# Adaptive-norm attention and expert layer: block 0 projected first, products of zeros ahead of it, output scaled by halves of the dimensions, last expert by single tiles

## What is computed

```python
mod = (silu(c) @ wmod).reshape(4, 6, 1, 128)
sa, ca, ga, sb, cb, gb = (mod[:, i] for i in range(6))
ga = (2 * (ga >= 0) - 1) * maximum(abs(ga), 0.25)     # gb likewise
h = layernorm(x) * (1 + ca) + sa
x = x + ga * attention(h)      # 16 heads of 64, 4 k/v heads, softcap 30, window of 128 tokens
h = layernorm(x) * (1 + cb) + sb
x = x + gb * experts(h)        # 8 experts, top 1, at most 512 tokens each, 128 -> 512 -> relu -> 128, biases b1, b2
```

## Time and profile before

| | |
|---|---|
| median of 3 runs | 460.33 us (460.16 to 461.42) |
| time of the profiled execution | 464.12 us |
| its span, first to last instruction | 462.3 us |
| TensorE busy | 413.0 us, 89% of the span |
| ScalarE, GpSimd, VectorE busy | 299.7, 309.5 and 285.5 us |
| mean granted TensorE clock | 0.964 |
| granted clock, 362 to 382 and 382 to 390 us | 0.73 and 0.50 |

### The profile page before, as it was taken

How to read it: one execution, slowest core, us unless ns; L and a number is a source line. 1 busy time by engine, 2 the same in 40 slices (tenths; PEclk the granted TensorE clock), 3 DMA queues, 4 the chain that set the end, 5 groups by cost and what they waited for, 6 DMA issues and landing times. The chain is left out here.

```text
span 462.3 us, 14917 instructions
## 1 busy us (share of the span) xinstructions
PE 413.0 (89%) x5608; PEld 291.8 (63%) x5608; DVE 285.5 (62%) x846; ACT 299.7 (65%) x537; POOL 309.5 (67%) x495
## 2 busy tenths in 40 slices
PE   2889999999999999999999999999989722899980
PEld 1756666665767676676766666767656512799970
DVE  4547566766776868486776756775767651246531
ACT  3788677768786868777777868776746430564520
POOL 4444757778787878687878757786869771065573
PEclk9999999999999999999999999999999955999996
DMA  8166602000110111020202101221210046971110
GB/s 240 69 214 239 198 12 81 26 31 28 45 48 26 57 51 31 37 60 36 67 29 83 47 30 32 65 64 32 83 43 24 30 127 207 353 227 36 38 47 21
DMA packets 32494, 37.14 MB, mean 80 GB/s; under 512 B 3634, under 2 KB 28727, under 8 KB 32424
## 3 DMA queue, kind: packets, MB, share of 16 engines
q1 hardware_dynamic: 28920, 27.43, 19.4%
q0 software_dynamic: 3072, 8.37, 5.0%
q10 hardware_dynamic: 432, 0.40, 0.4%
HBM read 15.69 MB, written 16.91 MB: 71 GB/s over the span
## 5 line engine op out<-in xcount | busy, mean ns | idle before, releaser
L899 DVE COPY_PREDICATED own<-before,turns 128x1024 f32<-128x1024 uint32 x56 | 68.8, 1229 | 47.5 <-PE turns L447 47.4
L1226 POOL TENSOR_TENSOR OL<-O,OH 128x512 fp32r<-128x512 f32 x64 | 81.7, 1284 | 17.9 <-ACT OH L730 17.9
L1218 POOL TENSOR_SCALAR_AFFINE_SELECT PM<-PR 128x1024 f32<-128x1024 f32 x64 | 70.5, 1101 | 10.8 <-ACT PR L724 10.7
L718 ACT ACTIVATE PR<-own 128x1024 f32<-128x1024 f32 x64 | 65.4, 1022 | 17.9 <-DVE own L899 17.9
L724 ACT ACTIVATE PR<-PR 128x1024 f32<-128x1024 f32 x64 | 67.1, 1048 | 0.1
L443 PE MATMUL own<-Q,K 64*32 64x128 f32 (+3 forms) x896 | 58.7, 441 | 2.5 <-ACT PR L718 2.0
L447 PE MATMUL turns<-Q,K 64*32 64x128 f32 (+3 forms) x896 | 57.4, 429 | 0.0
L930 DVE TENSOR_TENSOR O<-turns,R 128x512 f32<-128x512 f32 x64 | 43.0, 682 | 17.2 <-PE turns L486 17.0
L1262 POOL DMA_INDIRECT sorted_rows<-PAY,slot_i x32 | 34.7, 1085 | 12.3 <-issue 11.5
L704 ACT ACTIVATE Q<-turns 128x512 f32<-128x512 f32 x64 | 38.2, 598 | 7.0 <-PE turns L369 5.8
L447 PEld LDWEIGHTS turns<-Q,K 64*32 64x32 f32 x896 | 36.6, 107 | 9.5
(11 more groups left out here) (192 smaller groups left out, 1009.8 us busy)
## 6 DMA issues: line engine op xcount, KB each, us to landing
sorted_rows<-empty_row SPq DMA_DIRECT2D x8, 776.0 KB, 5.8
VM<-V SPq DMA_DIRECT2D x56, 64.0 KB, 2.1
out_dram<-PAY SPq DMA_DIRECT2D x32, 64.0 KB, 1.8
w_stage<-w_dram SPq DMA_DIRECT2D x8, 256.0 KB
Q<-sorted_rows SPq DMA_DIRECT2D x2, 776.0 KB, 8.1
PR<-sorted_rows SPq DMA_DIRECT2D x2, 776.0 KB, 9.7
x_sb<-sorted_rows SPq DMA_DIRECT2D x2, 776.0 KB, 9.2
x_sb<-x_dram SPq DMA_DIRECT2D x3, 512.0 KB, 5.8
```

The costliest lines, as they stand in the source:

```text
L718: act.activation(pr, own[:, :, :].rearrange("p a n -> p (a n)"), ACT.Tanh, scale=SCORE_SCALE).then_inc(tanhed, 1)
L899: dve.copy_predicated(own[:, :, :].rearrange("p a (r n) -> p (a r) n", n=P), before[:, :].bitcast(U32).unsqueeze(1).to_broadcast([P, 2 * R ...
L1218: pool.affine_select(out=PM[:, u % P_RING, :].rearrange("p (r n) -> p r n", n=P), in_=PR[:, u % P_RING, :].rearrange("p (r n) -> p r n", n ...
L1226: pool.tensor_tensor(OL[:, t % 2, c, :], O[:, t % 2, c, :], OH[:, t % 2, c, :].bitcast(F32), ALU.subtract).then_inc(ol_done, 1)
```

## The change

Four things are changed.

1. **Block 0 first.** TensorE projects K, Q1, Q0 (its groups 1 and 0) and V of block 0 before it transposes block 1; the guards `and e + ... > 1` take these calls out of the loop. VectorE measures tiles 0 and 1 ahead of silu, and everything for block 0 comes ahead of the measuring of tiles 2 and 3. Weights are loaded and split in the order K, Q0, V, Q1. `prepare_mod` moves to the next round. Semaphores of the gates are merged.
2. **Products of zeros.** `run_idle` multiplies 128 x 128 zeros by zeros into bank 5, which nobody reads: twice 512 columns before the columns product, 256 columns after the rows product, 512 columns after the transposes of block 0.
3. **Scaling by halves of the dimensions.** `scale`, `high_o` and `low_o` take half x of the head dimension for all tokens in place of half c of the tokens. Both banks are free only after both halves; `out_project` starts when the first half of the second tile is there.
4. **Last expert.** Its 512 rows are finished in four tiles of 128 in four banks, into memory of its own (`VM`), so without the wait for expert 5's stores; gate * b2 + x is prepared before.

```diff
@@ split and loads
-        SPLIT_K, SPLIT_Q1, SPLIT_Q0, SPLIT_V, SPLIT_O1, SPLIT_O0 = range(6)
+        SPLIT_K, SPLIT_Q0, SPLIT_V, SPLIT_Q1, SPLIT_O1, SPLIT_O0 = range(6)
...
+        last_banks = [turns[:, n, :] for n in (4, 5, 0, 1)]
@@ attend, out_project
-                freed[n] = scaled, 2 * t + 1
-                freed[n + 1] = scaled, 2 * t + 2
+                freed[n] = freed[n + 1] = scaled, 2 * t + 2
...
-                pe.wait_ge(oh_done, 4 * k + 4)
                 for i in range(2 * REP):
+                    if i % REP == 0:
+                        pe.wait_ge(oh_done, 4 * k + 3 + i // REP)
...
-                pe.wait_ge(ol_done, 4 * k + 4)
                 for i in range(2 * REP):
+                    if i % REP == 0:
+                        pe.wait_ge(ol_done, 4 * k + 3 + i // REP)
@@ TensorE, start
+            def run_idle(times, width):
+                n, ps = take("idle")
+                for i in range(times):
+                    pe.matmul(ps[:, 0:width * P].rearrange("p (a n) -> p a n", n=P), zeros[:, :],
+                              zeros[:, :].unsqueeze(1).to_broadcast([P, width, P]), start=True, stop=True)
+            pe.wait_ge(consts, 1)
+            run_idle(2, 4)
...
+            run_idle(1, 2)
             pe.wait_ge(consts, CONSTS)
+            turn_x(0)
+            run_idle(1, 4)
+            project_k(0)
+            project_q(0, 1)
+            project_q(0, 0)
+            project_v(0)
             for e in range(-16, TILES - 4, 2):
-                if is_tile(e + 12):
+                if is_tile(e + 12) and e + 12 > 1:
                     project_v(e // 2 + 6)
...
-                if is_tile(e + 16):
+                if is_tile(e + 16) and e + 16 > 1:
                     turn_x(e // 2 + 8)
@@ TensorE, experts
+            def down_last():
+                e = EXPERTS - 1
+                pe.wait_ge(w2_in[e], 16)
+                pe.wait_ge(relu_done, FC * (e + 1))
+                for s in range(ST):
+                    if s < 2:
+                        pe.wait_ge(b2_added, 2 * (e - 1) + s + 1)
+                    for f in range(FC):
+                        last = pe.matmul(last_banks[s][:, 0:P], hidden[e % 2][:, f, s * P:(s + 1) * P], w2_sb[e][:, f, :],
+                                         start=(f == 0), stop=(f == FC - 1))
+                    last.then_inc(down_done, 1)
@@ VectorE, scale
-            def scale(t, c):
+            def scale(t, x):
...
-                inverse = R[:, :].rearrange("p (r n) -> p r n", n=P)[:, :, HALVES[c]].unsqueeze(1).to_broadcast([P, 2, REP, HALF])
-                dve.tensor_tensor(O[:, t % 2, c, :].rearrange("p (x r n) -> p x r n", x=2, n=HALF),
-                                  bank["pv", t][:, c, :].rearrange("p (x r n) -> p x r n", x=2, n=HALF), inverse, ALU.mult).then_inc(scaled, 1)
+                half = slice(x * 2 * P, (x + 1) * 2 * P)
+                inverse = R[:, :].rearrange("p (r c n) -> p c r n", c=2, n=HALF)
+                dve.tensor_tensor(O[:, t % 2, :, half].rearrange("p c (r n) -> p c r n", n=HALF),
+                                  bank["pv", t][:, :, half].rearrange("p c (r n) -> p c r n", n=HALF), inverse, ALU.mult).then_inc(scaled, 1)
@@ VectorE, start
             dve.memset(turns[:, 0:4, :], 0.0).then_inc(banks_cleared, 1)
+            measure1(0)
+            measure1(1)
+            gather1(0)
+            gather1(1)
             prepare_silu()
+            split_low(SPLIT_K)
+            keep_columns()
+            full_x(0)
+            low_x(0)
+            split_low(SPLIT_Q0)
+            split_low(SPLIT_V)
+            keep_gate()
+            measure1(2)
+            measure1(3)
+            gather1(2)
+            gather1(3)
+            split_low(SPLIT_Q1)
@@ VectorE and GpSimd, last expert
+            def prepare_last():
+                rw = rows[EXPERTS - 1]
+                dve.wait_ge(rows_in[EXPERTS - 1], 16)
+                dve.tensor_tensor(more_rows, rw[:, :, ROW_G:ROW_G + P], b2_row[:, EXPERTS - 1, :].unsqueeze(1).to_broadcast([P, ST, P]),
+                                  ALU.mult).then_inc(more_done, 1)
+                dve.wait_ge(more_done, 1)
+                dve.tensor_tensor(more_rows, more_rows, rw[:, :, ROW_X:ROW_X + P], ALU.add).then_inc(more_done, 1)
+            def finish_last():
...
+                for s in range(ST):
+                    dve.wait_ge(down_done, 2 * e + s + 1)
+                    dve.tensor_tensor(last_rows[:, s, :], last_banks[s][:, 0:P], rows[e][:, s, ROW_G:ROW_G + P],
+                                      ALU.mult).then_inc(g_scaled, 1)
+                    dve.wait_ge(g_scaled, 2 * e + s + 1)
+                    dve.tensor_tensor(last_rows[:, s, :], last_rows[:, s, :], more_rows[:, s, :], ALU.add).then_inc(x_added, 1)
...
+            prepare_last()
             finish(EXPERTS - 2)
-            finish(EXPERTS - 1)
+            finish_last()
...
+            for s in range(ST):
+                pool.wait_ge(x_added, 2 * (EXPERTS - 1) + s + 1)
+                deliver(EXPERTS - 1, s)
```

More of the change, by code:

```diff
@@ L48 @@
 HOME = {
-    ("columns",): 4, ("rows",): 2,
+    ("idle",): 5, ("columns",): 4, ("rows",): 2,
     ("before", 0, 0): 3, ("before", 0, 1): 1, ("before", 1, 0): 0, ("before", 1, 1): 3,
@@ L183, in build @@
         b2_row = V[:, 0:4, :].rearrange("p a (b n) -> p (a b) n", n=P)
+        more_rows, last_rows = (VM[:, 2 * n:2 * n + 2, :].rearrange("p a (b n) -> p (a b) n", n=P) for n in range(2))
         done_rows = [at[:, :].rearrange("p (s d) -> p s d", s=ST) for at in (sumsT, R)]
```

110 lines of the change are left out of this document (54 added, 56 removed).

## The result

The change made the kernel slower: **462.95 us** (461.48 to 463.32, ten runs) against 460.44 (459.53 to 461.91, ten runs), a ratio of 1.0036 (1.0024 to 1.0049), 2.5 us above no change and 4 us above the upper end of my range. The profiled execution has a time of 463.02, a span of 461.3 and a mean granted clock of 0.958; before it was 0.964, and all but one of its ten runs show 0.958. On the three chips of the experiments where the kernel before takes 461 us, its 105 runs show 0.963 to 0.970.

A forecast was written before the change was run, and what follows sets the result against it. TensorE, busy 89% of the span, was taken to bound the long middle, leaving the start, the last attention tile and the last expert. Gains 1.8 + 0 + 1.9 = 3.7 us from 460.33 gave 456.6 us, range 454.7 to 458.9.

The forecast's parts named there:

- Part 1, start of block 0: Start of TensorE: XL of block 0 ready at 10.85, first real product at 11.1 instead of 14.10, 3.0 us earlier.
- Part 1, "Block 1, which now comes after": Price of block 0 first: block 1's transposes start at 15.75 against 13.78, two microseconds later.
- Part 1, "The clock": Start: gain 1.8, midway between 1.1 and 2.55, depending on whether the level is high at the rows product; bounds 0 to 3.0.
- 1.1 for this case: Start, without the higher clock level at the rows product: third Q copy at 18.5 instead of 19.60, 1.1 us gained.
- 2.55: Start gain if the level is already high at the rows product, which saves another 1.45 with zero product and transposes.
- The first rival: Start: the zeros raise the clock before block 0; gain 2.55 + 1.9, time 455.9 us; chance 0.20.
- The rival "slower": TensorE's queue ahead of the columns product: zeros last longer than their cover, 6.6 us lost, 463.2 us; chance 0.05.
- "Whatever the start gains passes through whole": The long middle is TensorE's with unchanged products, so any start gain reaches the end and the middle gives nothing itself.
- Part 2: 0 predicted: Scaling by halves: small changes hidden, out projection 0.5 earlier behind the last tile but GpSimd busy; 0, between −0.5 and +0.6.
- the term of 1.9 us: Last expert: GpSimd runs through, last store at 453.85 instead of 455.77; gain 1.9 us, bounds 0.3 to 2.2.
- "the wait for the stores of expert 5": Last expert: VectorE started only at 449.60, held by those stores, whose rows it overwrites; the new memory needs no such wait.
- The sum: Whole kernel: 1.8 + 0 + 1.9 = 3.7 us faster than the median 460.33, giving 456.6 us; forecast chance 0.52.

The follow-up runs named there:

- c_before: The kernel before, unchanged, run and profiled again: 461.02 us, ratio 0.9996; its profile is the reference for shifts.
- p1_fill: Part 1 alone on the kernel before, with three more zero products in the holes around block 1's transposes: 464.29 us, 0.9979 (third chip, before 465.14).
- a_fill: The change plus three 512-column zero products, two behind block 0's V and one behind block 1's transposes: 460.80 us, ratio 1.0000 against the kernel before.
- b_scale_pad: Part 2 alone on the kernel before, plus four 32-column zero products at the start of TensorE: 464.12 us, 0.9981 (third chip, before 465.14).
- e_gate: p1_fill_gate once more, on a fifth chip: 464.26 us, ratio 0.9988 against the kernel before at 465.30.
- p1_fill_gate: p1_fill with tiles 2 and 3 measured ahead of the gate's five small operations: 464.16 us, ratio 0.9986 against the kernel before.
- b_scale: Part 2 alone (scaling by halves of the dimensions) on the kernel before: 461.95 us, ratio 1.0016.
- c_after: The change again, on a third chip where the end is late: 464.09 us, ratio 0.9973 against the kernel before at 465.14.
- d_after: The change again, on a fourth chip beside its own parts: 461.59 us, ratio 1.0024 against the kernel before.
- a_early: The change with tiles 2 to 5 measured ahead of block 0's `full_x`: 461.22 us, ratio 1.0006 against the kernel before.
- a_early_pair: a_early without part 3, the last expert finished in two pairs as before: 459.77 us, ratio 0.9991 against the kernel before.

## Why the prediction was wrong, point by point

**Part 1, start of block 0: right within 0.4 us.** XL is ready at 11.27 (10.85 + 0.42; predicted 10.85), first product 11.42 (11.1).

**Part 1, "Block 1, which now comes after": 0.75 us short.** Transposes at 16.50, not 15.75: VectorE reached tiles 2 and 3 at 12.86, much as foreseen, but XN began on GpSimd's results only at 15.48, where I had 14.7. GpSimd's four operations took 1.8 us, from 13.65 to 15.44, where I had 1.5 from 13.2.

**Part 1, "The clock": the step that failed.** It gave the level two states for the whole start, low or high, and took a gain midway, 1.8, with bounds 0 to 3.0. It never asked what the level would do in the holes which its own numbers contain: at the higher level it let the 24 products of block 0 end by 14.0, with the next work at 15.75. I took that as harmless since ScalarE sets the pace. It is the hole in which, with the wait for the Q bank behind it, the level falls, and then Q2, the next block's transposes and projection run at 1.2 GHz. Measured in place of the gain of 1.8: a loss of 1.41 at the first tanh against the profile that the prediction was worked from (25.84 against 24.43), and of 1.96 against `c_before`.

The terms can be told apart. Against that same 24.43, `p1_fill`, with the lower level at the rows product and no fall, gains 0.34 where the prediction had 1.1 for this case, and `a_fill`, with the higher level there, gains 1.66 where it had 2.55. Both are short by 0.8 or 0.9, about what block 1's transposes are late. The change's profile lies 1.75 below `p1_fill`, and that is the fall. 1.1 − 0.76 − 1.75 = −1.41. And 24.43 is the latest of the seven first tanhs with this start, so part of the 1.1 was luck of that one profile.

The first rival put the rise ahead of the rows product. In four of the twelve profiles with zeros it is there, and block 0 then starts 1.34 us earlier (10.08 against 11.42), near the 1.45 that it gave. Its time of 455.9 is not reached, with the fall or, in `a_fill`, without it (1.0000). The rival "slower" gave 463.2, close to the 462.95 measured, but its condition did not hold: the two zero products took 3.78 us and ended at 4.83, and the columns product waited for its DMA until 5.26. That the time came near is luck.

The Trainium skill ("TensorE: Matmul & The Clock Gate", Part 1) was used for half of what it says: that activity releases the throttle. The trace agrees, block 0 at 0.12 us a product. But that section also makes throttled the default state, and this trace agrees with that as well, with 0.64 in the stretch behind the hole.

**"Whatever the start gains passes through whole": right to 355 us, wrong behind it.** The constant shift shows it up to the last tanh. Then the second fall, at 364, takes 1.1 to 1.8 us of it back in some executions, and where the experts begin the profiles differ by 2.2 us: from the copy of the last out projection to VectorE's first row of expert 0 it is 33.1 us in `b_scale_pad`, 34.4 in `c_before` and 35.3 in `a_fill`. The level is back up there 24, 26 and 28 us behind that copy, so it is likely the cause. So even the repaired start is worth 0.1%, with 1 in its interval: `e_gate` 0.9988, `p1_fill_gate` 0.9986 (0.9971 to 1.0002).

**Part 2: 0 predicted, +0.7 on one chip and −0.9 on another measured.** `b_scale` alone is 1.0016 on one chip, where its profile has the stop at 43 us, and `b_scale_pad` 0.9981 on another; its own effects in the traces are the 0.3 us wait of the K projection, whose bank 1 I had overlooked (it is covered by a wait for a tanh right behind), and the out projection 0.4 earlier, which GpSimd hides as I said. I can't give it a value of its own.

**Part 3: the term of 1.9 us was sized on one late execution.** The earlier trace rows come from the profile that lay 3.7 us above the median, and I subtracted the whole of it from the median. In an execution near the median the hole does not exist (`c_before`), and the part gives −0.2, for the slowed store, where 1.9 was predicted. Where the end is late it does save about 1.9 us, which is not the case that it was computed for. The mechanism was named wrongly too: "the wait for the stores of expert 5" does not explain a late second pair, nor one in code that has no such wait. What the first profile of before waited for, there for its first pair, is open. GpSimd had issued expert 5's last store by 444.6, five microseconds before the pair began, and in `c_before` such a store lands 2.2 us after its issue (median), so the stores are an unlikely answer there too.

**The sum.** Predicted −3.7; by the traces of the change and `c_before` +2.0 at the first tanh, +1.6 at VectorE's first row of expert 0 and +1.8 at the last store, and 2.5 by the median. Of the 2.0, a microsecond can be the moment at which the level first rose in either profile.

## What to carry to other kernels

An edit that closes one hole of TensorE by finishing earlier opens another further on; ask of each hole of a microsecond or more that is left whether the granted clock survives it, and read the clock column run by run, since it hints at such a loss where a single profile may not have it, though it gives neither the first rise nor the time. Two profiles of the same start differ by 1.7 us in their first tanh here, so measure an effect from an event that both have just ahead of it, such as block 0's first product, and not from the start of the program. Before a term is built on a wait, see whether the profiled execution is near the median: one that stands 3.7 us above it carries waits that the median doesn't have. A gain of 2 us at the start must be followed to the end, through each place at which TensorE waits.

## What the runs showed of the hardware that was not expected

- Products of zeros do raise the clock: block 0 at 0.12 us a product from 11.42 on, where before the same products took 0.22 until 19.36. Behind waits of 2.10 and 1.52 us it was down again for 6.8 us, behind 1.43 and 1.52 in `c_after` and 1.49 and 1.52 in `d_after` for 3.4; the wait of 1.52 alone left it up in `a_early` and `a_early_pair`. Three more zero products in the holes held it.
- The clock column is blind to the low level at the start: it reads 1.00 from 10 to 20 us in the kernel before, while products follow at 1.2 GHz. In all twenty profiles it shows a low level only after a first rise.
- An indirect store's issue on GpSimd took 1.48 us instead of 0.97 while VectorE ran the second 128x512 operation of `prepare_last` and, without a pause, the finishing of expert 6 beside it. With the two moved it took 0.97, and two later stores beside them 1.18 and 1.02. Which of VectorE's operations slows a store is not shown.
- On two of the five chips of the experiments the last products of the program were handed on late in all six profiles (waits of 2.2 to 4.5 us), and the kernel before takes some 4.5 us more there (465.14 and 465.30). The cause is open.
- TensorE stopped for 1.05 us inside a group of products at 43 us, in two kernels of twenty, with nothing named as releaser. Open too.
